# Head attention of a two-layer decoder: score peaks by row groups of four heads, two products per maximum, and the inverse of the sums on ScalarE

## The reference

```python
def _L1_xattn_ref(query, key, value, Wq, bq, Wk, bk, Wv, bv, Wo, bo):
    D_MODEL = 128
    H = 16
    D_K = D_MODEL // H
    B, Sq, _ = query.shape
    def proj(x, W, b):
        y = x @ W.T + b
        return y.reshape(B, -1, H, D_K).transpose(0, 2, 1, 3)
    q = proj(query, Wq, bq)
    k = proj(key, Wk, bk)
    v = proj(value, Wv, bv)
    scores = jnp.einsum('bhqd,bhkd->bhqk', q, k) / jnp.sqrt(jnp.float32(D_K))
    attn = jax.nn.softmax(scores, axis=-1)
    ctx = jnp.einsum('bhqk,bhkd->bhqd', attn, v)
    ctx = ctx.transpose(0, 2, 1, 3).reshape(B, Sq, D_MODEL)
    return ctx @ Wo.T + bo
...
x = x + _L1_xattn_ref(_layernorm(x, axis=-1), ctx_1024, ctx_1024, L1_xattn_Wq, L1_xattn_bq, ...)
```

## Time and profile before

| what | value |
|---|---|
| runs (us) | 1846.52, 1855.25, 1854.69 |
| profiled execution, span (us) | 1852.36, 1850.6 |
| PE busy | 1601.3 us, 87% |
| weight load busy | 1189.1 us, 64% |
| DVE busy | 1285.3 us, 69% |
| ACT busy | 862.9 us, 47% |
| POOL busy | 760.7 us, 41% |
| mean granted TensorE clock | 0.947 of full |
| maxima of P on DVE (line 1573) | 672 of 677 ns, 447.9 us |
| products P on PE (line 1367) | 672 |

### The profile page before, as it was taken

The page is one execution under the profiler, slowest core; times in us unless marked ns, Lnnn a source line. Parts: engine busy times, 40 slices in busy tenths (PEclk is TensorE's granted clock), DMA queues, the critical chain, the costliest instruction groups (busy, mean ns, idle before and its releaser), DMA issues. The chain is left out here.

```text
span 1850.6 us, 43148 instructions
## 1 busy us (share of the span) xinstructions
PE 1601.3 (87%) x15260; PEld 1189.1 (64%) x15260; DVE 1285.3 (69%) x1971; ACT 862.9 (47%) x1262; POOL 760.7 (41%) x753
## 2 busy tenths in 40 slices
PE   4687698859999966765999999999999999749998
PEld 2222366639999923434777777777777777448887
DVE  2596254537878759957777777777777777349998
ACT  2224233322222224333666666666666666425444
POOL 0592000027787729812333333333333332038876
PEclk8899799979999989878999999999999999859999
DMA  2000788412121000026655555555555554021211
GB/s 67 1 0 0 199 235 237 128 43 87 38 74 55 2 1 1 0 58 145 143 136 133 133 133 134 134 134 134 135 134 135 133 134 102 1 75 53 74 62 40
DMA packets 52306, 169.53 MB, mean 92 GB/s; under 512 B 12514, under 2 KB 23650, under 8 KB 52243
## 3 DMA queue, kind: packets, MB, share of 16 engines
q1 hardware_dynamic: 49938, 156.42, 33.8%
q10 hardware_dynamic: 2304, 12.29, 2.3%
HBM read 91.15 MB, written 1.04 MB: 50 GB/s over the span
## 5 line engine op out<-in xcount | busy, mean ns | idle before, releaser
L1573 DVE TENSOR_REDUCE hat_tops<-banks 128x1 f32<-128x500 f32 x672 | 447.9, 677 | 133.0 <-PE banks L1367 132.7
L1474 ACT ACTIVATE hat_pb<-banks 125x896 f32<-125x896 f32 x384 | 331.2, 916 | 145.6 <-PE banks L1386 144.3
L1367 PE MATMUL banks<-hat_kh,hat_qm 128*128 128x500 f32 x672 | 311.7, 465 | 19.0 <-DVE hat_tops L1573 17.4
L1519 POOL TENSOR_TENSOR hat_kl<-hat_kf,hat_kh 128x500 fp32r<-128x500 f32 x96 | 121.1, 1262 | 486.5 <-DMA hat_k<-hat_kh 296.4
L1386 PEld LDWEIGHTS banks<-hat_q,hat_k 128*125 128x125 f32 x1536 | 218.7, 188 | 39.5 <-issue 24.4
L1386 PE MATMUL banks<-hat_q,hat_k 128*125 128x224 f32 x1536 | 236.0, 276 | 5.4 <-issue 4.4
L1377 PE MATMUL banks<-hat_pb,hat_vs 125*27 125x168 f32 (+1 forms) x6144 | 186.3, 262 | 0.1
L1377 PEld LDWEIGHTS banks<-hat_pb,hat_vs 125*27 125x27 f32 (+1 forms) x6144 | 135.6, 98 | 72.9 <-ACT hat_pb L1474 39.0
L1367 PEld LDWEIGHTS banks<-hat_kh,hat_qm 128*128 128x128 f32 x672 | 128.2, 191 | 63.6 <-DVE hat_tops L1573 45.1
L1022 ACT ACTIVATE ffn_rg<-banks 128x448 f32<-128x448 f32 x128 | 69.7, 545 | 168.9 <-PE banks L981 168.9
L1667 POOL CAST moe_hh<-moe_hf 128x448 fp32r<-128x448 f32 x144 | 115.9, 823 | 64.0 <-ACT moe_hf L1726 63.9
(11 more groups left out here) (259 smaller groups left out, 3198.1 us busy)
## 6 DMA issues: line engine op xcount, KB each, us to landing
hat_k<-hat_kh SPq DMA_DIRECT2D x256, 187.5 KB, 4.7
hat_ct<-ctxT SPq DMA_DIRECT2D x32, 750.0 KB, 6.1
hat_k<-hat_kl SPq DMA_DIRECT2D x128, 187.5 KB, 4.5
ctx_cx<-ctx SPq DMA_DIRECT2D x32, 672.0 KB
ctx_cd<-ctxT ACTq DMA_DIRECT2D x16, 750.0 KB, 8.9
moe_cb<-all_expert_weights SPq DMA_DIRECT2D x9, 896.0 KB, 4.7
ffn_cb<-all_expert_weights SPq DMA_DIRECT2D x8, 896.0 KB, 4.6
moe_raw<-Mw SPq DMA_DIRECT2D x18, 256.0 KB, 5.0
```

Of the source, the lines that this page charges most:

```text
L1367: peak_out.inc(nc.tensor.matmul(g.bank(PK + m % 2)[:, 0:SB], qm[u][:].rearrange("p h i -> p (h i)")[:, r * 128:r * 128 + 128], kh[u][:, c ...
L1474: exped.inc(nc.scalar.activation(pb[t % 4][:].rearrange("p (n i) -> p n i", n=2), g.ps[0:SW, 2 * (t % 2):2 * (t % 2) + 2, 0:2 * QW], ACT.E ...
L1519: k_low.inc(nc.gpsimd.tensor_tensor(kl[:, cols], kf[:, cols], kh[u][:, cols].bitcast(F32), ALU.subtract))
L1573: peaked.inc(v.tensor_reduce(tops[:, r, n:n + 1], g.bank(PK + m % 2)[:, 0:SB], AX_X, ALU.max))
```

## The change

The masked queries now hold four heads instead of sixteen (`hat_qm` of 128 x 4 x 56): partition block 32g keeps the four heads of group g. A peak product uses only the 32 partitions of one group as rows of the array, and gives two heads (112 of the columns) for 500 keys. Two such products, of groups 2a and 2a+1, go to banks 4 and 5, and one maximum on 112 partitions reads both banks (2 x 500 columns) and writes two maxima. So there are 24 products in 12 pairs (PEAKS = 12), and 12 maxima. A pair waits that the maximum of the pair before it is read, and all pairs that `shifted` of the batch before is done, since bank 5 (LAST) is also that of the turned maxima. `PLACES` has 3, 2, 2, 3, 2 and 0 places in the six steps. The top product is moved ahead of K in step 5, and W of step 5 behind K.

DVE's reciprocal is gone. ACT takes the logarithm of the sums and the exponential of its negative (`invert`, at the head of step 3, and once behind the last slot), and DVE's product is in step 4. The product K of step 3 now waits for the logarithm (`logged`), since that reads bank 7.

```diff
@@ -1275,10 +1275,10 @@
-    ROWS = H * L // 128
-    PEAKS = ROWS * 3
+    ROWS, RW = 2 * G, 2 * L
+    PEAKS = ROWS // 2 * 3
     IT = ST // 2
-    PLACES = [(0, 1, 2, 3), (1, 2, 3), (0, 1, 2, 3), (1, 2, 3), (0, 1, 2, 3), (0, 1, 2)]
+    PLACES = [(0, 1, 3), (1, 3), (1, 3), (0, 1, 3), (1, 3), ()]
...
-        qm = [sb(f"qm{u}", [128, H, L], F32R) for u in range(2)]
+        qm = [sb(f"qm{u}", [128, HG, L], F32R) for u in range(2)]
...
-        tops, top = sb("tops", [128, ROWS, 3]), sb("top", [128, ROWS])
-        om, on, rc = sb("om", [128, 3, L]), sb("on", [128, 2, L]), sb("rc", [128, 2, L])
+        tops, top = sb("tops", [RW, ROWS, 3]), sb("top", [RW, ROWS])
+        om, on, rc = sb("om", [128, 3, L]), sb("on", [128, 2, L]), sb("rc", [128, 2 * L])
...
-        peak_of = lambda m: (m % ROWS, m // ROWS)
+        peak_of = lambda m: (m % 4 // 2, m % 2, m // 4)
...
                 def sum_weights(q):
                     picked.wait(pe, q)
-                    inverted.wait(pe, q - 1)
+                    logged.wait(pe, q - 1)
...
                     m = BEFORE[i] + PLACES[i].index(place)
-                    r, c = peak_of(m)
+                    a, t, c = peak_of(m)
                     if m == 0:
                         qm_made.wait(pe, q)
-                    if r == 0:
+                    shifted.wait(pe, q - 1)
+                    if m % 4 == 0:
                         k_high.wait(pe, q, c + 1)
-                    peaked.wait(pe, *((q, m - 1) if m >= 2 else (q - 1, PEAKS)))
-                    if m == 1:
-                        shifted.wait(pe, q - 1)
-                    peak_out.inc(nc.tensor.matmul(g.bank(PK + m % 2)[:, 0:SB], qm[u][:].rearrange("p h i -> p (h i)")[:, r * 128:r * 128 + 128],
-                                                  kh[u][:, c * SB:(c + 1) * SB], start=True, stop=True))
+                    peaked.wait(pe, *((q, m) if m >= 1 else (q - 1, PEAKS)))
+                    for k in range(2):
+                        rows = slice(64 * a + 32 * k, 64 * a + 32 * k + 32)
+                        mm = nc.tensor.matmul(g.bank(PK + k)[0:RW, 0:SB], qm[u][rows, 2 * t:2 * t + 2, :].rearrange("p h i -> p (h i)"),
+                                              kh[u][rows, c * SB:(c + 1) * SB], start=True, stop=True)
+                    peak_out.inc(mm)
...
                         if maxima:
                             peak(p - 1, 1 - u, i, 2)
+                            if i == IT - 1:
+                                topped.wait(pe, p - 1)
+                                top_out.inc(nc.tensor.matmul(g.bank(LAST)[96:96 + ROWS, 0:RW], top[:], c_["minus_ident"][0:RW, 0:RW], start=True, stop=True))
...
+                def invert(q):
+                    sum_out.wait(act, q)
+                    normed.wait(act, q - 1)
+                    logged.inc(nc.scalar.activation(rc[:], g.bank(MISC)[:, 0:2 * L], ACT.Ln))
+                    logged.wait(act, q)
+                    inverted.inc(nc.scalar.activation(rc[:], rc[:], ACT.Exp, scale=-1.0))
+
                 def slot(p, u, h, keys, maxima, sums):
                     for i in range(IT):
+                        if i == 3 and sums and from_third(p):
+                            invert(p - 3)
...
-                        qm_made.inc(nc.gpsimd.tensor_tensor(qm[u][:], spread(g.xn[:, bass.ds(p * L, L)], 1, H), spread(c_["head_of"], 2, L), ALU.mult))
+                        qm_made.inc(nc.gpsimd.tensor_tensor(qm[u][:], spread(g.xn[:, bass.ds(p * L, L)], 1, HG), spread(c_["head_in_group"], 2, L), ALU.mult))
...
-                    sum_out.wait(dve, q)
-                    inverted.inc(v.reciprocal(rc[:], g.bank(MISC)[:, 0:2 * L].rearrange("p (n i) -> p n i", n=2)))
                     inverted.wait(dve, q)
-                    normed.inc(v.tensor_tensor(ot[:, :, bass.ds(q * L, L)], on[:], rc[:], ALU.mult))
+                    normed.inc(v.tensor_tensor(ot[:, :, bass.ds(q * L, L)], on[:], rc[:].rearrange("p (n i) -> p n i", n=2), ALU.mult))
...
-                            if i == 3:
+                            if i == 4:
                                 divide(p - 3)
...
-                                peaked.inc(v.tensor_reduce(tops[:, r, n:n + 1], g.bank(PK + m % 2)[:, 0:SB], AX_X, ALU.max))
+                                a, t, c = peak_of(m)
+                                peaked.inc(v.tensor_reduce(tops[:].rearrange("p (a k t) c -> p a k t c", a=2, k=2)[:, a, :, t, c],
+                                                           g.ps[0:RW, PK:PK + 2, 0:SB], AX_X, ALU.max))
```

More of the change, by code:

```diff
@@ L1300, in head_attention @@
         (qm_made, k_full, v_out, v_copied, q_spread, peak_out, peaked, topped, top_out, shifted, k_out, k_high, k_low,
-         scored, exped, summed, own, picked, sum_out, inverted, normed) = (flow(n, k) for n, k in (
+         scored, exped, summed, own, picked, sum_out, logged, inverted, normed) = (flow(n, k) for n, k in (
             ("qm_made", 1), ("k_full", 3), ("v_out", 3), ("v_copied", 3), ("q_spread", 1), ("peak_out", PEAKS), ("peaked", PEAKS),
             ("topped", 1), ("top_out", 1), ("shifted", 1), ("k_out", 3), ("k_high", 3), ("k_low", 3),
-            ("scored", ST), ("exped", ST), ("summed", ST), ("own", 1), ("picked", 2), ("sum_out", 1), ("inverted", 1), ("normed", 1)))
+            ("scored", ST), ("exped", ST), ("summed", ST), ("own", 1), ("picked", 2), ("sum_out", 1), ("logged", 1), ("inverted", 1), ("normed", 1)))
         projected, filled, added, biased = sem("projected"), sem("filled"), sem("added"), sem("biased")
@@ L1403, in some_keys @@
                         v_copied.wait(pe, p - 1)
-                        inverted.wait(pe, p - 3)
+                        logged.wait(pe, p - 3)
                     else:
@@ L1426, in slot @@
                             peak(p - 1, 1 - u, i, 2)
+                            if i == IT - 1:
+                                topped.wait(pe, p - 1)
+                                top_out.inc(nc.tensor.matmul(g.bank(LAST)[96:96 + ROWS, 0:RW], top[:], c_["minus_ident"][0:RW, 0:RW], start=True, stop=True))
                             if i < 3:
                                 values(p - 1, 1 - u, i)
-                        if keys and i >= 3 and i < IT - 1:
+                        if keys and i >= 3:
                             some_keys(p, u, h, i - 3)
@@ L1438, in slot @@
                             weigh(p - 3, 1 - u, ST - 1)
[L1439 to L1443, removed]
                         if i == 2 and sums and from_third(p):
@@ L1461, in _ @@
             def _(act):
-                give(act, v_copied, k_full, k_high, exped)
+                give(act, v_copied, k_full, k_high, exped, logged, inverted)
                 for c in range(CH):
@@ L1493, in _ @@
                 staged(act, B, slot)
+                invert(B - 1)
             @block.gpsimd
@@ L1551, in divide @@
                         dve.wait_ge(q_in, 12 * 16)
-                    sum_out.wait(dve, q)
-                    inverted.inc(v.reciprocal(rc[:], g.bank(MISC)[:, 0:2 * L].rearrange("p (n i) -> p n i", n=2)))
                     inverted.wait(dve, q)
-                    normed.inc(v.tensor_tensor(ot[:, :, bass.ds(q * L, L)], on[:], rc[:], ALU.mult))
-                give(dve, peaked, topped, shifted, own, picked, inverted, normed)
+                    normed.inc(v.tensor_tensor(ot[:, :, bass.ds(q * L, L)], on[:], rc[:].rearrange("p (n i) -> p n i", n=2), ALU.mult))
+                give(dve, peaked, topped, shifted, own, picked, normed)
                 def slot(p, u, h, keys, maxima, sums):
@@ L1571, in slot @@
                                     topped.wait(dve, q - 1)
-                                r, n = peak_of(m)
-                                peaked.inc(v.tensor_reduce(tops[:, r, n:n + 1], g.bank(PK + m % 2)[:, 0:SB], AX_X, ALU.max))
+                                a, t, c = peak_of(m)
+                                peaked.inc(v.tensor_reduce(tops[:].rearrange("p (a k t) c -> p a k t c", a=2, k=2)[:, a, :, t, c],
+                                                           g.ps[0:RW, PK:PK + 2, 0:SB], AX_X, ALU.max))
                     if maxima:
@@ L1583, in slot @@
                         shifted.inc(v.tensor_tensor(q3[1 - u][96:96 + ROWS].rearrange("p g c -> p (g c)").rearrange("p (r x) -> p r x", r=ROWS),
-                                                    spread(g.bank(LAST)[96:96 + ROWS, 0:128], 1, ROWS),
-                                                    spread(c_["own_chunk"][96:96 + ROWS, 0:ROWS], 2, 128), ALU.mult))
+                                                    spread(g.bank(LAST)[96:96 + ROWS, 0:RW], 1, ROWS),
+                                                    spread(c_["own_chunk"][96:96 + ROWS, 0:ROWS], 2, RW), ALU.mult))
                 staged(dve, B, slot)
```

## The result

The changed kernel takes 1950.06 us (median of 4 runs, 1948.88 to 1950.88) against 1852.61 for the kernel before on the same chip: ratio 1.0529, 95% interval 1.051 to 1.0549. The forecast was 1935 and slower. The profiled execution has a span of 1947.6 us, 97.0 more than before.

The account below looks back on a forecast made before the run. PE's own sequence of pieces was taken to bound the kernel. Slot 22.98 to 25.39 us, +2.41 over 31 periods, +75, and +5 for the first slot, on 1852.4: 1932, with 2.3 for the median 1935; range 1882 to 1990.

Parts of the forecast that it names:

- The turnaround: From pair to pair: maximum 1.18 us, its end to the next load 0.06, load to maximum 0.54; at least 1.78.
- The changes of tile shape: On PE around each pair: 0.10 us before the next load may start and 0.10 for an exposed first load.
- The slot: Period of the top products in the loop: 25.39 us against 22.98 before, summed pair by pair.
- five kinds of distance within the slot: Pair to pair on PE: P S 1.78 us, P S V 1.92, P W S 1.96, P W sum 1.90, P S K 1.88.
- its end: PE's last pieces of a slot, P W S S top K W: 4.53 us.
- free changes: Rival: changing to row blocks costs nothing on PE; slot 24.0 us, time 1887 us; chance 0.19.
- products in a line: Rival: a pair's two products run one after the other; slot 28.2 us, time 2021 us; chance 0.11.
- The clock: Something unseen that slows the kernel, as a lower clock in PE's new gaps; chance 0.01.
- the first top: End of the first slot with maxima, forecast +5 us later from its turnarounds and a cold PE.
- The inverse on ACT: Logarithm and exponential on ACT replace DVE's 857 ns reciprocal in each slot; costed at nothing.
- The faster rival: Handshake doesn't bind and PE is relieved: slot 20.9 us, time 1788 us; needs a turnaround of 1.5; chance 0.05.
- The rival in which gain and loss cancel: Turnaround between 1.5 and 1.65 with free changes: slot 22.5 to 23.3 us, within 10 us of before; chance 0.04.

Follow-up runs that it names:

- same_rows: Changed kernel with both products of a pair reading the same block of 32 rows; 2176.13 us, ratio 1.1764.
- half_max: Changed kernel with maxima reading only 2 x 250 of the 2 x 500 columns; 1902.89 us, ratio 1.0287.
- full_rows: Changed kernel with each product of a pair over all 128 partitions, so no 32-row blocks; 1984.06 us, ratio 1.0726.
- row_blocks_alone: Changed kernel without pairs: 24 single 32-row products, one 112x500 maximum each, banks 4 and 5 in turn, top behind the last; 2178.51 us.
- full_half_max: Changed kernel with products over all 128 partitions and maxima of 2 x 250 columns; 1900.31 us, ratio 1.0273.

## Why the prediction was right

- **The turnaround.** 1.18 + 0.06 + 0.54 = 1.78 forecast; 1.20 + 0.05 + 0.53 = 1.78 measured, and 1.80 on the mean from pair to pair. Extrapolating the maximum's length from two shorter ones was 1.7% short.
- **The changes of tile shape.** Forecast 0.20 for each change of shape, from column strips (0.10 until the next load may start, 0.10 for a first load that is not hidden); the row blocks alone show 0.37 for both sides of a P between two S, against 0.40 as I had it.
- **The slot.** 25.39 forecast, 25.47 at the upper clock. It is right piece by piece and not by errors that cancel: the five kinds of distance within the slot came within 0.03 us, and only its end, 4.53 forecast and 4.70 measured, was 0.17 short. No run puts the old order of step 5 back, so what that reordering is worth in the changed kernel is not shown. The rivals of free changes (24.0) and of products in a line (28.2; same_rows has 28.1 to 28.3) are excluded, each by a run of its own.
- **The clock.** The step that was missed: I gave a lower clock in PE's gaps 0.01. It is 14 of the 97 us (9.9 in six slots, 3.7 in the first period). The slot was 2.7 us short over 31 periods and the first top 1.1; against that, the median lies 0.6 above the profiled execution and not 2.3. Together that is the 15 by which 1935 was short.
- **The inverse on ACT.** Priced at nothing because DVE was idle for 26% of a slot, and that reasoning was wrong for the changed kernel, though the sum was not hurt: it had no reciprocal in it. Put back, it costs 72 us, 25 by its own delay and the rest with the clock. The logarithm brought no load of an activation table: nine in the whole program, before and after. A busy share can't tell what an instruction costs that stands between two links of a chain. The handshake made DVE a link, and this edit is what kept the change from being 9% slower.
- **The faster rival** needed a turnaround of 1.5. In half_max it is 1.26, and the kernel is still 2.9% slower, so that rival's own condition was too weak: it left out the changes of shape.
- **The rival in which gain and loss cancel** was worked out wrongly. By the sum of the other rivals (eleven distances and an end of 4.4), a turnaround of 1.5 to 1.65 gives a slot of 20.9 to 22.6; the slot of 22.5 to 23.3 needs 1.65 to 1.72. The measured 1.78 excludes it either way.

## What to carry to other kernels

Giving both buffers of a pair to one producer step halves the number of handshakes but lays each bare; work out reader time plus both latencies, and set it against the distance at which the steps stand in the other engine's order. Products on different parts of the array's rows run side by side, but strewn one by one or in pairs among full-array ones they gave back what that saved: 0.37 us for each change of shape and back, against 0.21 for each pair. When a chain becomes the bound, every instruction in the queue between its links gets a price, whatever the engine's idle share.

## What the runs showed of the hardware that I had not expected

The granted clock did not go by PE's busy share over long stretches. It stayed at 1.00 with whole rows and 186.6 of 200 us busy (full_rows), and was 0.93 with 32-row products and 192.75 of 200 (row_blocks_alone). What stood before the falls were pauses of PE: 0.67 to 0.75 us in the changed kernel, 0.98 in row_blocks_alone. In half_max, with 32-row products and no pause over 0.3 us, the clock stayed at 1.00 through the loop.

But pauses alone don't explain it. The waits of PE for a maximum, 920 to 1600 us, first the changed kernel with its six falls, then full_rows without one:

```profile
PE banks L1368 <- DVE hat_tops L1581: 36.2, 52, 0.8
...
PE banks L1368 <- DVE hat_tops L1581: 44.3, 50, 1.0
```

full_rows waits as often in each slot and longer. The first slots with maxima point the same way. half_max and full_half_max differ in the rows of their products alone, and PE pauses there for 0.78 and 0.77 us between pairs. Here is half_max, then full_half_max:

```profile
850.00:875.00 25.00, 20.82 (x60) 10.74 (x58) 8.31 (x13) 6.75 (x10) 6.13 (x8) 0.50 0.16 45
...
850.00:875.00 25.00, 19.41 (x125) 12.81 (x126) 11.32 (x18) 10.18 (x15) 7.47 (x8) 1.00 0.32 82
```

With whole rows the clock is at its upper level from 850.2 us on, with row blocks only from 881.5.

The Trainium skill (TensorE: Matmul & The Clock Gate, "What's actually happening") has the clock set by how busy PE has been recently. The pauses before the falls agree with it. By that alone the changed kernel should have kept its clock better than full_rows, and these traces show the opposite. Which property of a product on few rows counts (its rows, or the changes of shape around it) stays open: no run had the one without the other.
